# A graph attention layer on one core: edge sums written to the softmax chain's partitions, a chain of six slots, aggregation 15 slots behind

## What is computed

```python
h = (x @ W.T).reshape(n, H, D)
h_src = h[src]
h_dst = h[dst]
alpha = jnp.einsum('ehd,hd->eh', h_src, a_src) + jnp.einsum('ehd,hd->eh', h_dst, a_dst)
enc = jax.nn.relu(edge_attr @ edge_W.T + edge_b).reshape(-1, H, D)
alpha = alpha + jnp.sum(enc * h_dst, axis=-1)
alpha = jnp.where(alpha >= 0, alpha, 0.2 * alpha)
amax = jax.ops.segment_max(alpha, dst, num_segments=n)
ex = jnp.exp(alpha - amax[dst])
denom = jax.ops.segment_sum(ex, dst, num_segments=n)
attn = ex / jnp.maximum(denom[dst], 1e-10)
out = jax.ops.segment_sum(h_src * attn[..., None], dst, num_segments=n)
```

## Time and profile before

| | us |
|---|---|
| median of 3 runs | 2183.68 (2181.82 to 2191.77) |
| span of the profiled execution | 2179.1 |
| PE busy | 2044.9 (94%) |
| DVE busy | 1545.8 (71%) |
| POOL busy | 1279.5 (59%) |
| ACT busy | 1277.0 (59%) |

### The profile page before, as it was taken

The page is one execution under the profiler, slowest core; times in us unless marked ns, Lnnn a source line. Parts: engine busy times, 40 slices in busy tenths (PEclk is TensorE's granted clock), DMA queues, the critical chain, the costliest instruction groups (busy, mean ns, idle before and its releaser), DMA issues. The chain is left out here.

```text
span 2179.1 us, 40886 instructions
## 1 busy us (share of the span) xinstructions
PE 2044.9 (94%) x11567; PEld 1610.2 (74%) x11568; DVE 1545.8 (71%) x3782; ACT 1277.0 (59%) x3507; POOL 1279.5 (59%) x1434
## 2 busy tenths in 40 slices
PE   7799999999999999999999585999999999999997
PEld 5566667666666666666766485998888888888886
DVE  8589999999999999999998878344333334344332
ACT  4688888878888887877887465332222333322222
POOL 2377777777777777777777000455555555555554
PEclk9899999999999999999999757999999999999998
DMA  8766555655655555565564967122222222222221
GB/s 258 218 184 178 171 176 174 179 171 169 182 172 174 178 176 173 169 180 170 171 181 133 323 226 132 39 34 34 36 34 36 34 34 34 34 34 35 35 36 24
DMA packets 164043, 279.58 MB, mean 128 GB/s; under 512 B 36736, under 2 KB 115361, under 8 KB 163778
## 3 DMA queue, kind: packets, MB, share of 16 engines
q0 software_dynamic: 66720, 149.75, 28.9%
q1 hardware_dynamic: 88618, 121.01, 17.5%
q10 hardware_dynamic: 8568, 7.25, 1.0%
HBM read 240.94 MB, written 36.97 MB: 128 GB/s over the span
## 5 line engine op out<-in xcount | busy, mean ns | idle before, releaser
L647 POOL DMA_INDIRECT arena<-h_tab,src x880 | 845.0, 960 | 312.0 <-issue 242.2
L1611 ACT ACTIVATE arena<-psum,arena 128x128 f32<-128x128 f32 x840 | 239.4, 368 | 558.1 <-PE psum L1551 558.1
L813 PE MATMUL psum<-arena 128*128 128x256 f32 x1760 | 478.8, 395 | 1.2 <-issue 1.2
L834 PE MATMUL psum<-arena 128*128 128x264 f32 x1760 | 475.7, 394 | 0.7 <-DVE arena L925 0.7
L1551 PEld LDWEIGHTS psum<-arena 128*128 128x128 f32 x3360 | 386.2, 193 | 44.3 <-DVE arena L1634 25.3
L1551 PE MATMUL psum<-arena 128*128 128x128 f32 x3360 | 404.1, 279 | 8.4 <-DVE arena L1634 6.5
L834 PEld LDWEIGHTS psum<-arena 128*128 128x128 f32 x1760 | 321.9, 191 | 96.1 <-issue 45.4
L1585 PE MATMUL psum<-arena 128*128 x1680 | 384.3, 382 | 0.6
L813 PEld LDWEIGHTS psum<-arena 128*128 128x128 f32 x1760 | 318.4, 191 | 81.9 <-issue 37.0
L1585 PEld LDWEIGHTS psum<-arena 128*128 128x128 f32 x1680 | 311.3, 190 | 45.6 <-issue 5.0
L905 DVE SCALAR_TENSOR_TENSOR arena<-arena,a_dst,psum 128x512 f32<-128x512 f32 x440 | 325.5, 740 | 14.0 <-ACT arena L713 6.3
(11 more groups left out here) (225 smaller groups left out, 1939.4 us busy)
## 6 DMA issues: line engine op xcount, KB each, us to landing
arena<-rel_list SPq DMA_DIRECT2D x110, 512.0 KB
arena<-in_W SPq DMA_DIRECT2D x16, 1024.0 KB, 12.5
arena<-h_tab,src POOLq DMA_INDIRECT x880
arena<-ea_slots SPq DMA_DIRECT2D x440, 27.0 KB
arena<-in_x SPq DMA_DIRECT2D x12, 896.0 KB, 8.8
h_tab<-arena SPq DMA_DIRECT2D x6, 924.0 KB, 6.6
out_rows<-arena SPq DMA_DIRECT2D x5, 896.0 KB, 5.0
xn<-arena ACTq DMA_DIRECT2D x5, 896.0 KB, 6.7
```

The lines of the kernel that those rows point to most:

```text
L647: pool.indirect_dma_start(rows[:, s % RING, k, :], None, d.h_tab[:, :], bass.IndirectOffsetOnAxis(ap=c.src[:, s * U + k:s * U + k + 1], ax ...
L813: last = nc.tensor.matmul(ps[:, HDT + x, y * UE:(y + 1) * UE], hj[:, (s // 2 * 2 + y) % HJ, x * P:(x + 1) * P], oht[:, half % OT, (u + y) ...
L834: last = nc.tensor.matmul(ps[:, AGG + a % 2, 0:HS], oh[:, a % OH, k, :], rows[:, a % RING, k, :], start=(k == 0), stop=(k == U - 1))
L1611: last = nc.scalar.activation(hT[:, b, h * P:(h + 1) * P], ps[:, UP + 2 * b + n, h % 4 * P:(h % 4 + 1) * P], ACT.Gelu, bias=b1_now[:, b, h ...
```

## The change

The feature sums no longer go by edges. `block_ones` grows from 2 blocks of 32 columns to 8 blocks, one for each feature half x and each m of four column tiles, so that `reduce` writes heads and column tiles straight onto the 128 partitions on which the chain works: 32 matmuls of 128 columns in place of 8 of 512. ACT's new `take_sources` copies the source scores out of the gathered rows at slot 1, when the chunk's gathers have landed, and a 33rd matmul against the identity adds them to the sums in PSUM. ACT copies the sums (128 columns), DVE rectifies out of PSUM into that copy. `to_edges`, `to_heads` and `logits` are gone; every later piece stands three slots sooner, and LAG is 15. The slots of `select` stay. SP's loads at the end wait for the last reduction instead of the last logits. `block_ones` moves to the end of the arena.

```diff
-LAG = 2 * CS + 2
+LAG = 2 * CS - 1
...
-            pool.iota(bo_row.rearrange("p (x r h) -> p x r h", x=2, h=H), [[-4, 2], [0, 4], [1, H]], base=0, channel_multiplier=0, **ia).then_inc(consts_made, 1)
+            pool.iota(bo_row.rearrange("p (x m r h) -> p x m r h", x=KH, m=4, h=H), [[-4, KH], [-64, 4], [64, 4], [1, H]], base=0, channel_multiplier=0, **ia).then_inc(consts_made, 1)
...
-            sp.wait_ge(alpha_made, 2 * NCH)
+            sp.wait_ge(red_done, NCH)
+            sp.wait_ge(first_kept, NCH)
...
+            def take_sources(ch):
+
+                for half in (2 * ch, 2 * ch + 1):
+                    act.wait_ge(gathered[half % GATS], (half // GATS + 1) * 4 * U * 16)
+                if ch:
+                    act.wait_ge(red_done, ch)
+                for u0, u1 in parts(ch):
+                    last = nc.scalar.copy(sources[:, u0 * U * H:u1 * U * H].rearrange("p (t h) -> p t h", h=H), ring(ch, u0, u1)[:, :, HD:HS])
+                last.then_inc(sources_taken, 1)
+
             def sums(ch):
+
                 act.wait_ge(red_done, ch + 1)
-                nc.scalar.copy(red, ps[:, SM, :]).then_inc(red_taken, 1)
-
-            def by_head(ch):
-                act.wait_ge(turned, ch + 1)
-                nc.scalar.copy(leaky, ps[:, SM, 0:P]).then_inc(leaky_made, 1)
+                nc.scalar.copy(leaky, ps[:, SM, 0:P]).then_inc(sums_taken, 1)
...
+                for ch in due(t, 1):
+                    take_sources(ch)
                 for ch in due(t, 2):
                     sums(ch)
+                for ch in due(t, 4):
+                    factor(ch)
                 for ch in due(t, 5):
-                    by_head(ch)
-                for ch in due(t, 9):
+                    exponent(ch)
+                for ch in due(t, 6):
                     weights(ch)
...
-                for x in range(2):
-                    for g in range(4):
-                        last = nc.tensor.matmul(ps[32 * g:32 * g + 32, SM, :], c.block_ones[:, x * 32:(x + 1) * 32], renc[:, (4 * ch + g) % RENC, x, :],
-                                                start=(x == 0), stop=(x == 1))
-                last.then_inc(red_done, 1)
+                for x in range(KH):
+                    for m in range(4):
+                        for g in range(4):
+                            nc.tensor.matmul(ps[32 * g:32 * g + 32, SM, 0:P], c.block_ones[:, (4 * x + m) * 32:(4 * x + m + 1) * 32],
+                                             renc[:, (4 * ch + g) % RENC, x, m * P:(m + 1) * P], start=(x == 0 and m == 0), stop=False)
+                pe.wait_ge(sources_taken, ch + 1)
+                nc.tensor.matmul(ps[:, SM, 0:P], sources, c.ident[:, :], start=False, stop=True).then_inc(red_done, 1)
...
             def tile_ends(ch):
+                dve.wait_ge(sums_taken, ch + 1)
+                nc.vector.scalar_tensor_tensor(leaky, ps[:, SM, 0:P], 0.2, leaky, ALU.mult, ALU.max).then_inc(leaky_made, 1)
                 dve.wait_ge(leaky_made, ch + 1)
...
-                for ch in due(t, 3):
-                    logits(ch)
-                for ch in due(t, 5):
-                    tile_ends(ch)
-                for ch in due(t, 6):
+                for ch in due(t, 3):
                     chain_tiles(ch)
-                for ch in due(t, 7):
+                for ch in due(t, 4):
                     fall_factors(ch)
                     shift(ch)
-                for ch in due(t, 8):
+                for ch in due(t, 5):
                     node_scale(ch)
                 if t % CS in AHEAD_OF and SELECTED * 2 <= t + AHEAD_OF[t % CS] < SLOTS:
                     select((t + AHEAD_OF[t % CS]) // 2)
```

More of the change, by code:

```diff
@@ L161, in prepare @@
         p_by32_f, p_by8_f, p_low = (work.take(1) for _ in range(3))
-        bo_row, low_row = work.take(2 * 32), work.take(P)
+        bo_row, low_row = work.take(KH * 4 * 32), work.take(P)
         dst_rows, src_rows, rel, src_f, ea_rows = (lists.take(SG * n).rearrange("p (g e) -> p g e", g=SG) for n in (UE, UE, UE, UE, (EF + 1) * UE))
@@ L600, in edges @@
         rows = take(RING * U * HS).rearrange("p (r k n) -> p r k n", r=RING, k=U)
-        at, end = REST_AT + EA_WORDS, ARENA
+        at, end = REST_AT + EA_WORDS, ARENA - KH * 4 * 32
         oh = take(OH * UE).rearrange("p (b k n) -> p b k n", b=OH, k=U)
-        red = take(512)
-        alpha, leaky, fwd, top, ex = (take(P) for _ in range(5))
+        sources, leaky, fwd, top, ex = (take(P) for _ in range(5))
         link = take(2 * (P + 1)).rearrange("p (b e) -> p b e", b=2)
@@ L835, in aggregate @@
                 last.then_inc(agg_done, 1)
-            def to_edges(ch):
-                pe.wait_ge(red_taken, ch + 1)
-                for m in range(4):
-                    last = nc.tensor.transpose(ps[:, SM, m * P:(m + 1) * P], red[:, m * P:(m + 1) * P], c.ident[:, :])
-                last.then_inc(back_done, 1)
-            def to_heads(ch):
-                pe.wait_ge(alpha_made, 2 * ch + 2)
-                nc.tensor.transpose(ps[:, SM, 0:P], alpha, c.ident[:, :]).then_inc(turned, 1)
             def chain(ch):
@@ L871, in _ @@
                 for ch in due(t, 4):
-                    to_heads(ch)
-                for ch in due(t, 7):
                     join(ch)
@@ L878, in _ @@
                     aggregate(a)
-                for ch in due(t, 8):
+                for ch in due(t, 5):
                     to_rows(ch)
                     factors(ch)
-                for ch in due(t, 2):
-                    to_edges(ch)
-                for ch in due(t, 6):
+                for ch in due(t, 3):
                     chain(ch)
@@ L1008, in _ @@
                 a = t - LAG
-                if t % CS == 0 and 0 <= a + 1 < SLOTS:
+                last_of_chunk = (a + 1) % CS == CS - 1
+                if last_of_chunk and 0 <= a + 1 < SLOTS:
                     message(a + 1)
@@ L1012, in _ @@
                     product(t - 1)
-                if t % CS and 0 <= a + 1 < SLOTS:
+                if not last_of_chunk and 0 <= a + 1 < SLOTS:
                     message(a + 1)
@@ L1020, in _ @@
                     take_sums(a - 1, js)
+                for ch in due(t, 2):
+                    tile_ends(ch)
                 for ch in due(t, 3):
-                    logits(ch)
-                for ch in due(t, 5):
-                    tile_ends(ch)
-                for ch in due(t, 6):
                     chain_tiles(ch)
-                for ch in due(t, 7):
+                for ch in due(t, 4):
                     fall_factors(ch)
                     shift(ch)
-                for ch in due(t, 8):
+                for ch in due(t, 5):
                     node_scale(ch)
@@ L1707, in program @@
         c.a_dst = sb("a_dst", [P, KH])
-        c.block_ones = sb("block_ones", [P, KH * 32])
+        c.block_ones = c.arena[:, ARENA - KH * 4 * 32:ARENA]
         c.low = sb("low", [P, H])
```

28 lines of the change are left out of this document (7 added, 21 removed).

## The result

The changed kernel takes 2212.63 us (median of 4 runs, 2210.87 to 2214.39) beside 2183.32 us of the kernel before on the same chip: a ratio of 1.0128, with a 95% interval of 1.0103 to 1.0153. The forecast was 2201 us in a range of 2176 to 2226, slower by over 0.5%. So the sign held, and the loop that was forecast, and the size was 12 us short. The profiled span is 2209.5 us, 30.4 us more than before.

A forecast was written before the change was run, and what follows sets the result against it. The DVE and PE loop (20.05 us) bounds the kernel, POOL (20.0) close behind. New loop 9.3 + 11.4 = 20.7, taken as 20.6: + 22 + 2 - 7 = + 17 on 2179.1, 2196, plus 4.6: 2201 us, range 2176 to 2226.

The forecast's parts named there:

- the loop that was forecast: Loop between DVE and PE sets the pace at 20.4 to 20.9 us, 2190 to 2216 us; chance 0.50.
- The bound: DVE from slot 2's sum to PE's to-rows transpose 9.3 us, PE from there to the next sum 11.4 us.
- The reduction: On PE, 64 short records in 16 rounds take 1.71 us as now, plus 0.03 us for staggered starts.
- Rival C's prices: In the reduction, short records cost 0.44 us a chunk more (2224 us, chance 0.12) or 1.7 (2289 us, 0.05).
- The slots: Chain pieces moved into slots 2, 3 and 4 beside DVE's comparisons; the loop goes from 20.05 to 20.7 us.
- 20.6 taken for a count of 20.7: Loop period rounded down: undisturbed periods lie a little under the count, and 0.09 us at the product may not show.
- Edges of the loop: Ahead of the third reduction + 2 us; behind the last reduction 21.7 us for 28.6, - 7 us.
- The lost cover: On PE, encodings no longer hidden beside small operations in their old slots: some 0.6 us of cover goes.
- Rivals A and B: First: POOL's gathers set the pace, 2170 us, chance 0.10; second: loop 20.1 to 20.35 us, 2182 us, chance 0.20.

The follow-up runs named there:

- e1: Changed kernel with DVE's target comparison of slot 4 moved to slot 6: 2626.0 us, where the kernel before takes about 2556 us.
- e2: Changed kernel with DVE's target comparison of slot 2 moved to slot 7: 2626.9 us, where the kernel before takes about 2556 us.
- e8: Changed kernel with the later pieces and lag put back to the old slots, new reduction kept: 2600.1 us, where the kernel before takes about 2556 us.
- e7: The changed kernel itself, unedited, as a control: 2623.39 us, on a chip where the kernel before takes about 2556 us.
- e12: Changed kernel with e11's cut reduction and the old slots and lag: 2254.9 us, where the kernel before takes 2182.2 us.
- e11: Changed kernel with its 64 short reduction records cut into four bursts of 16: 2289.6 us, where the kernel before takes 2182.2 us.
- e3: Changed kernel with PE's edge encodings moved from even to odd slots: 2600.8 us, where the kernel before takes about 2556 us.
- e10: The kernel before itself, unedited, as a control: 2563.66 us in its one run beside 2555.85 us.

## Why the prediction held, and where it was short

- **The bound.** The loop of DVE and PE, not POOL, sets the period: in undisturbed chunks 9.29 + 11.40 = 20.69 us, counted as 9.3 + 11.4. e1 and e2 show which part of DVE's stretch counts and which does not.
- **The reduction.** Taken as 0.03 us above before; measured 1.89 for 1.85 to the next matmul. Rival C's prices (0.44 and 1.7 us) did not come: four strips start some 7 ns apart, and rounds follow at 0.109 us. The Trainium skill ("TensorE: Matmul & The Clock Gate", section "Wait — 56ns, not 53.3ns?") gives about 62 ns per matmul with hardware decode off as the bound for short ones; nothing of it is seen here, since 64 records start within 1.68 us, 27 ns each. But the term was sized from undisturbed rounds. That 64 short records with their loads do not always flow was not in it. It cost 6.4 us on record, and is the mis-sized term; why the records stall stays open.
- **The slots.** The loop grew from 20.05 to 20.69 us, 0.64 by the prediction's own two counts, and both counts came out (9.29 and 11.40). This is read from the traces of the two kernels; no experiment isolates it. e8 against e7 (0.69) and e12 against e11 (0.72) are of that size, but over other waits, so that is luck as far as is known.
- **20.6 taken for a count of 20.7.** The undisturbed periods are 20.66 to 20.69. The rounding down was the wrong choice and cost 51 x 0.08 = 4 us. With the 6.4 us this is the 10 by which third to last reduction (1078.9) exceeds 1069; the last period was 17.66 for 18.3.
- **Edges of the loop.** 2.9 in front for + 2, a tail of 21.2 for 21.7. The 3.1 us behind the loop were counted as nothing and have no explained cause.
- **The sum of the misses.** The span is 2209.5 for 2196: 10 + 0.9 - 0.5 + 3.1 = 13.5 us. The runs' median lies 3.1 us over that span, not 4.6, which takes off 1.5 and leaves the 12. So the misses are small ones of both signs, most of them towards too fast.
- **The lost cover.** PE's stretch has the predicted length with two encodings at 0.52 us, and e3 shows that one beside the factors costs nothing (0.66 us with it and without). So the cover was lost as predicted, 0.52 us of it in slot 5. That moving the encodings would shorten the period by as much is not shown.
- **Rivals A and B.** POOL waits for aggregations (33.0 us in 64 times, 130 to 1210 us), and nobody waits for a gather after the first chunks but once; there was no slack that took up more than counted.

## What to carry to other kernels

When a dependency chain is moved into fewer slots, add up the other engine's path between its two meeting points as it will then stand, with everything queued ahead of the message that is waited for: busy shares fell on every engine here, and the time rose. A piece of work costs its full length if it stands behind the last wait of that path; ahead of a wait, it costs nothing as long as the wait is longer. And four times as many short matmuls for the same columns took no more time in 42 of 55 chunks here, but not in all: look for gaps in the trace. What breaks up the burst has a price of its own, 0.33 us a cut here, and the later end of the sums held up DVE by 2.3 and 2.5 us a chunk besides.

## What the runs showed of the hardware

- A burst of 64 short matmul records with 64 loads can lose time that no wait explains: 0.1 to 0.8 us in 13 of 55 chunks on record, and 5.8 us in the burst shown of e7. In bursts of 16 (e11, one chip) there was none; with the burst cut into two of 32 (e6) PE idled 2.0 us a chunk for 2.6. But the length alone does not decide: in e8 all 55 bursts of 64 together idle 0.3 us, nearly all of them starting at the lower clock behind 4 us in which PE waited. On record the first step over 125 ns stands behind the 57th to 60th record (in 11 of the 13), in e7 the first over 0.2 us is behind the 19th to 46th.
- In the trace on record a transfer of 16 KB on the queue that the profile calls "instruction" begins 0.97 to 1.24 us after the start of 8 of the 13 stretched reductions (at 357.0 us in the one shown). Of the 42 others two have one that begins 1.23 and 1.25 us after their start, and none has one between 0.7 and 1.2. Five of the 13 have none near. That suggests that instructions arrive too slowly, and a burst at half pace that does not idle (e8) would fit, but no run separates it.
- Where the kernel before takes 2556 us, signals of PE reach DVE, ACT and POOL late, 4.8 us after the end of the instruction that gives them in the chunk shown of e10. An instruction supply that runs dry does not explain this by itself, since PE goes on. The Trainium skill ("NOTIFIC — the notification-queue block", section "Overflow: three behaviours, one of which stalls the engine") says that the unit that writes the execution's records applies back pressure inside rather than lose one, and may so hold up an engine. Late signals and stalls where instructions are shortest would fit, but no run here leaves the records out. Which of the two it is, and why the chips differ, stays open.
- Once PE has idled in such gaps its clock falls: the 28 records behind the gaps in e7 take 1.94 us, at a granted clock of 0.50 (1.2 GHz), where 32 take 1.08 ahead of them at 1.00 (2.4 GHz). The windows view grants 0.92 over 300 to 1100 us for 1.00 on record.
